# A sixteen-step recurrence chunk split in two halves, with one set of matrix products between them

## The reference

```python
for t in range(T):                       # state S: [B, H, DK, DV]
    S = S * a[t]                         # decay, one number for each value channel
    kS = k[t] @ S                        # what the state holds for this key
    S = S + outer(k[t], beta[t] * (v[t] - kS))
    o[t] = q[t] @ S
```

## Time and profile before

| what | value |
|---|---|
| device time, median of 3 runs | 3930.03 us (3925.61 to 3930.99) |
| profiled execution | 3934.55 us, its span 3932.7 us |
| recurrence, 64 chunks | about 104 to 2367 us of the span |
| mean granted PE clock, as a share of full | 0.895 |
| DVE busy over the span | 3225.6 us (82%) |
| PE busy over the span | 3308.3 us (84%) |
| POOL busy over the span | 2378.6 us (60%) |

### The profile page before, as it was taken

One profiled execution on the slowest core, in us unless ns is written; L12 is line 12 of the kernel. 1 busy time (PEld: TensorE's weight loads), 2 busy tenths in 40 slices (PEclk: granted clock), 3 DMA queues, 4 the chain that ended last, 5 costly groups with the idle time before them and its releaser, 6 DMA issues. The chain is left out here.

```text
span 3932.7 us, 110963 instructions
## 1 busy us (share of the span) xinstructions
PE 3308.3 (84%) x45505; PEld 2330.9 (59%) x45505; DVE 3225.6 (82%) x6024; ACT 2050.2 (52%) x4682; POOL 2378.6 (60%) x2981
## 2 busy tenths in 40 slices
PE   6788888888888888888888855759999899898989
PEld 4565666656656566565665634536666567655765
DVE  4899999999999999999999993048888778747884
ACT  4344444444444444444444423238888789728982
POOL 0777787777777887778777772430011088608860
PEclk9788888889888888888988875879999999999999
DMA  2111111111111111111111104100000011101110
GB/s 79 43 35 42 39 36 35 39 39 42 31 40 38 39 40 31 42 38 37 36 29 39 36 25 134 45 23 2 2 2 2 17 31 42 32 20 28 41 35 27
DMA packets 156105, 139.05 MB, mean 35 GB/s; under 512 B 65207, under 2 KB 108435, under 8 KB 155343
## 3 DMA queue, kind: packets, MB, share of 16 engines
q1 hardware_dynamic: 153294, 129.25, 11.9%
q0 software_dynamic: 2304, 2.71, 0.2%
HBM read 96.12 MB, written 16.82 MB: 29 GB/s over the span
## 5 line engine op out<-in xcount | busy, mean ns | idle before, releaser
L1133 DVE TENSOR_TENSOR a_tmp<-a_h,banks 128x128 f32<-128x128 f32 (+14 forms) x960 | 721.3, 751 | 33.9 <-POOL a_h L908 4.0
L1139 DVE TENSOR_REDUCE a_h<-a_tmp 128x64 f32<-128x128 f32 (+14 forms) x960 | 723.0, 753 | 26.3
L908 POOL TENSOR_TENSOR a_h<-a_h,a_a 128x128 f32<-128x128 f32 (+11 forms) x768 | 587.6, 765 | 135.9 <-DVE a_h L1139 121.0
L893 POOL TENSOR_TENSOR a_st<-a_st,a_ab 128x512 f32<-128x512 f32 x256 | 327.0, 1277 | 0.0
L740 ACT ACTIVATE a_va<-banks 128x512 f32<-128x512 f32 x128 | 138.0, 1078 | 354.9 <-PE banks L543 354.9
L529 PEld LDWEIGHTS banks<-a_xseg,a_w_k 128*128 128x128 f32 x2048 | 256.9, 208 | 54.5 <-DVE a_h L1139 35.3
L1984 ACT ACTIVATE c_s<-c_s,c_low 128x384 f32<-128x384 f32 (+1 forms) x512 | 266.3, 579 | 19.0 <-DVE c_low L1928 13.5
L2029 POOL TENSOR_TENSOR c_qm<-c_qT,c_heads 128x512 f32<-128x512 f32 x32 | 33.3, 1040 | 396.1 <-PE banks L1853 395.7
L529 PE MATMUL banks<-a_xseg,a_w_k 128*128 128x128 f32 x2048 | 262.9, 292 | 11.5 <-DVE a_h L1139 6.6
L1928 DVE CUSTOM_DVE_ANT_0 c_s<-banks,c_band 128x384 f32<-128x384 f32 (+1 forms) x512 | 245.4, 517 | 23.6 <-PE banks L1853 23.6
L657 PE MATMUL banks<-a_wt,a_kt 32*64 32x64 f32 x8192 | 157.3, 251 | 115.3 <-DVE a_wt L1157 111.4
(11 more groups left out here) (298 smaller groups left out, 8234.4 us busy)
## 6 DMA issues: line engine op xcount, KB each, us to landing
a_ab<-decays SPq DMA_DIRECT2D x512, 128.0 KB, 2.9
d_Vs<-d_V SPq DMA_DIRECT2D x128, 128.0 KB, 2.3
sent<-k_nothing SPq DMA_DIRECT2D x40, 64.5 KB, 2.3
b_xe<-sent SPq DMA_DIRECT2D x8, 322.5 KB, 3.4
a_xseg<-xn SPq DMA_DIRECT2D x32, 70.0 KB, 2.5
xn<-a_xnT SPq DMA_DIRECT2D x8, 256.0 KB, 2.7
a_xrow<-in_L_attn_x SPq DMA_DIRECT2D x128, 16.0 KB, 1.8
x<-a_xrow SPq DMA_DIRECT2D x128, 16.0 KB
```

Source lines behind the costliest of these rows:

```text
L893: e.tensor_tensor(sv, sv, self.ab[:, 8 * n:8 * n + 8, :], ALU.mult).then_inc(*self.s_decay.at((g, n)))
L908: e.tensor_tensor(self.history(ch, t + 1)[:, :, 0:t], self.history(ch, t)[:, :, 0:t], at, ALU.mult).then_inc(*self.s_hist.at((g, t)))
L1133: e.tensor_tensor(prod, both, gram, ALU.mult).then_inc(*step.at((g, t, "product")))
L1139: e.tensor_reduce(self.results(ch, t), prod, AX.X, ALU.add).then_inc(*step.at((g, t, "w")))
```

## The change

`HC` = 8 takes the place of `HOLD`. A chunk now has two halves of eight steps. In a step the history goes back only to the start of the step's half, so L1133 and L1139 have at most 64 x 8 elements and POOL's history at most 32 x 7. Step 8 isn't computed as a step. In its place `dve_cross` transposes the updates of the first half into `Wt`, PE multiplies them by the Gram matrix of the first half against the second (`pe_cross`, into banks 6 and 7), DVE transposes the products into a new tile `X`, and a product and a sum make the first four columns of the second half. POOL makes the other four (`pool_cross`) and corrects the query part (`pool_query`, now three instructions). DVE does the decays of steps 9 to 11 as it does those of 1 to 3. Running products of the decays now restart in the middle of a chunk, so `pool_cumulate` has 7 steps of twice the width instead of 15, and `pool_second_half` and `pool_first_half` multiply the middle's decay in. ACT makes a masked copy of the Gram matrix (`act_cross_gram`) and copies a second set of decay rows.

```diff
-HOLD = 9
+HC = CK // 2
 HAND = 4
...
+    def pe_cross(self, e, q, s, ch):
+        g, xb = 2 * s + ch, self.c.bank(6, 2)
+        q.wait_ge(self.s_gx, s)
+        q.wait_ge(self.s_wm, g)
+        for ct in range(NCT):
+            for par in range(2):
+                x, at = 16 * par + 2 * ct, par * BANK + ct * DK
+                for bi in range(NB):
+                    rows = slice(bi * SEG, (bi + 1) * SEG)
+                    t = e.matmul(xb[rows, at:at + DK], self.Gx[rows, :, :, 8 * par + ct].rearrange("p z t -> p (z t)"),
+                                 self.Wt[rows, x:x + 2, :].rearrange("p h i -> p (h i)"), start=True, stop=True)
+        t.then_inc(*self.s_x.at(g))
...
     def pe_carry(self, e, q, g):
+        q.wait_ge(self.s_xt, g)
...
-                q.wait_ge(self.s_step, (g, HOLD, "w"))
+            self.pe_cross(e, q, s, 0)
+            if more:
                 for half in range(2):
...
+                self.pe_project_rows(e, q, "v", nxt, 0)
+            self.pe_cross(e, q, s, 1)
             if older >= 0:
                 self.pe_out(e, q, older)
             if more:
-                q.wait_ge(self.s_step, (g, HOLD, "w"))
-                for half in range(2):
-                    self.pe_project_rows(e, q, "v", nxt, half)
+                self.pe_project_rows(e, q, "v", nxt, 1)
             self.pe_carry(e, q, g)
...
+    def act_cross_gram(self, e, q, s):
+        q.wait_ge(self.s_evac, ("gram", s, 1))
+        if s:
+            q.wait_ge(self.s_x, 2 * s - 1)
+        e.activation(self.Gx[:], self.G1[:], ACT.Identity, scale=self.cst["first_half"][:, 0:1],
+                     bias=self.cst["first_half"][:, 1:2]).then_inc(*self.s_gx.at(s))
...
+            lo = t // HC * HC
+            at = self.a2[s % 2][:, :, ch * CK + t:ch * CK + t + 1].broadcast_to([P, 32, t - lo])
             q.wait_ge(self.s_step, (g, t - 1, "w"))
-            if t > HAND:
+            if t > lo + HAND:
                 q.wait_ge(self.s_hist, (g, t - 1))
-            e.tensor_tensor(self.history(ch, t + 1)[:, :, 0:t], self.history(ch, t)[:, :, 0:t], at, ALU.mult).then_inc(
+            e.tensor_tensor(self.history(ch, t + 1)[:, :, lo:t], self.history(ch, t)[:, :, lo:t], at, ALU.mult).then_inc(
                 *self.s_hist.at((g, t)))
...
+    def pool_first_half(self, e, q, s, ch):
+        g, part, c1 = 2 * s + ch, self.W[ch][:, :, ch * CK:ch * CK + HC], ch * CK + CK - 1
+        q.wait_ge(self.s_wm, g)
+        e.tensor_tensor(part, part, self.dc[s % 2][:, :, c1:c1 + 1].broadcast_to([P, 32, HC]), ALU.mult).then_inc(
+            *self.s_hist.at((g, "whole")))
...
+    def pool_second_half(self, e, q, s, ch):
+        g, rest, c0 = 2 * s + ch, self.P2[:, :, HC:, 0], ch * CK
+        both = self.P2[:, :, HC:, :].rearrange("p i t z -> p i (t z)")
+        q.wait_ge(self.s_prep, (g, "sub"))
+        q.wait_ge(self.s_cum, (s, HC - 1))
+        e.tensor_tensor(both, both, self.dc[s % 2][:, :, c0 + HC - 1:c0 + HC].broadcast_to([P, 32, CK]),
+                        ALU.mult).then_inc(*self.s_rest.at((g, "middle")))
+        q.wait_ge(self.s_rest, (g, "middle"))
+        q.wait_ge(self.s_dk, (g, 1))
+        e.tensor_tensor(rest, rest, self.dk[:, :, HC:], ALU.mult).then_inc(*self.s_rest.at((g, "second")))
+        q.wait_ge(self.s_rest, (g, "second"))
+        q.wait_ge(self.s_bv, s)
+        e.tensor_tensor(rest, self.bv[:, :, c0 + HC:c0 + CK], rest, ALU.subtract).then_inc(*self.s_rest.at((g, "less")))
...
+    def pool_cross(self, e, q, s, ch):
+        g, x, at = 2 * s + ch, self.X[:, :, HC + HAND:CK], HC + HAND
+        q.wait_ge(self.s_xt, g)
+        e.tensor_tensor(x, x, self.dk[:, :, at:], ALU.mult).then_inc(*self.s_cross.at((g, "mul")))
+        q.wait_ge(self.s_cross, (g, "mul"))
+        for odd in range(2):
+            e.tensor_tensor(self.history(ch, at + odd)[:, :, at + odd::2], self.P2[:, :, at + odd::2, 0], x[:, :, odd::2],
+                            ALU.add).then_inc(*self.s_rest.at((g, "late", odd)))
...
     def pool_query(self, e, q, s, ch):
-        g, dc, P2 = 2 * s + ch, self.dc[s % 2], self.P2
-        q.wait_ge(self.s_cum, (s, CK - 1))
-        q.wait_ge(self.s_prep, (g, "sub"))
-        e.tensor_tensor(P2[:, :, :, 1], P2[:, :, :, 1], dc[:, :, ch * CK:(ch + 1) * CK],
-                        ALU.mult).then_inc(*self.s_pq.at(g))
+        g, of_q, last = 2 * s + ch, self.P2[:, :, :, 1], HC - 1
+        q.wait_ge(self.s_xt, g)
+        q.wait_ge(self.s_rest, (g, "middle"))
+        e.tensor_tensor(of_q[:, :, HC:], of_q[:, :, HC:], self.X[:, :, CK + HC:], ALU.subtract).then_inc(*self.s_cross.at((g, "q")))
+        q.wait_ge(self.s_cross, (g, "q"))
+        e.tensor_tensor(of_q, of_q, self.dc[s % 2][:, :, ch * CK:(ch + 1) * CK], ALU.mult).then_inc(*self.s_cross.at((g, "decayed")))
+        q.wait_ge(self.s_cross, (g, "decayed"))
+        e.tensor_tensor(of_q[:, :, last], of_q[:, :, last], self.X[:, :, CK + last], ALU.subtract).then_inc(*self.s_pq.at(g))
...
             self.pool_rest(e, q, s, 0)
-            self.pool_history(e, q, s, 0, HAND, 8)
+            self.pool_history(e, q, s, 0, HAND, HAND + 1)
+            self.pool_second_half(e, q, s, 0)
+            self.pool_history(e, q, s, 0, HAND + 1, HC)
             if old >= 0:
                 self.pool_centre(e, q, old, 0)
-            self.pool_history(e, q, s, 0, 8, 10)
+            self.pool_first_half(e, q, s, 0)
+            self.pool_cross(e, q, s, 0)
             if old >= 0:
                 self.pool_centre(e, q, old, 1)
-            self.pool_history(e, q, s, 0, 10, 12)
             self.pool_query(e, q, s, 0)
             for n in range(4):
-                self.pool_history(e, q, s, 0, 12 + n, 13 + n)
+                self.pool_history(e, q, s, 0, HC + HAND + n, HC + HAND + n + 1)
                 self.pool_decay(e, q, g, n)
             self.pool_prepare(e, q, s, 1)
...
+            self.pool_history(e, q, s, 1, HAND, HAND + 1)
+            self.pool_second_half(e, q, s, 1)
+            for t in range(HAND + 1, HC):
                 self.pool_history(e, q, s, 1, t, t + 1)
                 if more:
-                    self.pool_cumulate(e, q, nxt, 2 * (t - HAND), 2 * (t - HAND) + 2)
+                    self.pool_cumulate(e, q, nxt, t - HAND - 1, t - HAND)
+            if more:
+                self.pool_cumulate(e, q, nxt, 3, 5)
+            self.pool_first_half(e, q, s, 1)
+            self.pool_cross(e, q, s, 1)
+            if more:
+                self.pool_cumulate(e, q, nxt, 5, HC)
             self.pool_query(e, q, s, 1)
             for n in range(4):
-                self.pool_history(e, q, s, 1, 12 + n, 13 + n)
+                self.pool_history(e, q, s, 1, HC + HAND + n, HC + HAND + n + 1)
                 self.pool_decay(e, q, g, n)
             if more:
...
+            lo = t // HC * HC
+            if t == HC:
+                self.dve_cross(e, q, s, ch)
+                continue
+            hist, prod = self.history(ch, t), self.tmp[:, :, :, 0:t + 1 - lo]
+            both = hist[:, :, lo:t + 1].rearrange("p (o i) j -> p o i j", o=1).broadcast_to([P, 2, 32, t + 1 - lo])
+            gram = self.gbank[:, t - 1, :, lo:t + 1].rearrange("p z (o j) -> p z o j", o=1).broadcast_to([P, 2, 32, t + 1 - lo])
+            if t == lo + 1 and lo:
+                q.wait_ge(self.s_mid, (g, "add"))
+            elif t > 1:
                 q.wait_ge(step, (g, t - 1, "w"))
-            if t == HAND:
-                q.wait_ge(self.s_rest, (g, "sub", 1))
-            if t > HAND:
+            if t == lo + HAND:
+                q.wait_ge(self.s_rest, (g, "late" if lo else "sub", 1))
+            if t > lo + HAND:
                 q.wait_ge(self.s_hist, (g, t - 1))
             e.tensor_tensor(prod, both, gram, ALU.mult).then_inc(*step.at((g, t, "product")))
-            if t < HAND:
-                at = self.abank[:, t, :].rearrange("p (i o) -> p i o", o=1).broadcast_to([P, 32, t])
+            if t < lo + HAND:
+                at = self.abank[:, t, :].rearrange("p (i o) -> p i o", o=1).broadcast_to([P, 32, t - lo])
                 q.wait_ge(step, (g, t, "product"))
-                e.tensor_tensor(hist[:, :, 0:t], hist[:, :, 0:t], at, ALU.mult).then_inc(*step.at((g, t, "decay")))
+                e.tensor_tensor(hist[:, :, lo:t], hist[:, :, lo:t], at, ALU.mult).then_inc(*step.at((g, t, "decay")))
             q.wait_ge(step, (g, t, "product"))
...
+    def dve_cross(self, e, q, s, ch):
+        g, x = 2 * s + ch, self.X[:, :, HC:HC + HAND]
+        q.wait_ge(self.s_step, (g, HC - 1, "w"))
+        q.wait_ge(self.s_hist, (g, HC - 1))
+        if g:
+            q.wait_ge(self.s_u, (g - 1, 3))
+        e.transpose(self.Wt[:].rearrange("p x i -> p i x"), self.W[ch]).then_inc(*self.s_wm.at(g))
+        q.wait_ge(self.s_x, g)
+        if g:
+            q.wait_ge(self.s_pq, g - 1)
+        e.transpose(self.X[:], self.c.bank(6, 2).rearrange("p (x i) -> p i x", i=32)).then_inc(*self.s_xt.at(g))
+        q.wait_ge(self.s_xt, g)
```

(11 more changed lines are left out.)

67 lines of the change are left out of this document (37 added, 30 removed).

## The result

| | before | after |
|---|---|---|
| median of the runs, us | 3930.51 (3925.61 to 3937.14, 4 runs) | 4322.32 (4314.57 to 4334.36, 4 runs) |
| ratio after / before | | 1.0998 [1.0968, 1.1029] |
| span of the profiled execution, us | 3932.7 | 4332.6 |

The change makes the kernel 10% slower. The forecast was 4180 us with a range of 4090 to 4300: the direction was right and so was most of the way it comes about, but the size was not, and the result lies outside the range.

What follows compares the result with a forecast made beforehand. DVE was taken as the bound (94% busy in the recurrence), PE close behind. 29 segments x 8.3 us more, plus 8 for the others, made 249 on 3934.55: 4184, forecast as 4180 us, range 4090 to 4300.

Steps and rivals of the forecast that it cites:

- DVE is spared 5 to 6 us a chunk, and doesn't get the time: Shorter products and sums save DVE 5 to 6 us a chunk, but it must wait mid-chunk for PE, then POOL.
- POOL in the first half: POOL's second-half products delay history 5, so step 7 ends 11.2 instead of 9.9 us after the chunk's products transpose.
- The middle of an even chunk: PE reaches the middle products 14.6 us after the chunk's products transpose, they take 2.3, and X comes at 18.2.
- After X POOL sets the pace: From X to the update transpose POOL's queue takes 10.4 us in even chunks, where DVE alone would need 8.3.
- The odd chunk's value rows: Half of the value rows, 5.0 us, stands before the middle products, which PE reaches 18.6 us after the products transpose.
- The prediction's first rival: Half clock: middle products cost 3.36 instead of 2.3 us, value rows 7.3 instead of 5.0; 4312 us, chance 0.11.
- The sum: A segment takes 36.8 + 42.2 = 79.0 us against 70.67, 8.3 more in each of 29 segments.
- The SBUF lock: Behind X, DVE and POOL instructions reading SBUF may hold each other: DVE up to 0.9 us a chunk, POOL 0.6.
- PE in time: Rival: PE waits for DVE at the middle in both chunks, 1.3 us a segment more, 3972 us, chance 0.06.
- The point from which the change pays: X 16.0 us after the products transpose in both chunks with POOL as forecast, 17.9 if POOL keeps up.
- rival 3: Faster: PE arrives early and POOL keeps up, so only DVE counts; 5.1 us less a segment, 3767 us, chance 0.04.

Runs made afterwards that it cites:

- the third experiment: Kernel after the change, with POOL's three second-half products moved from between history 4 and 5 to behind history 7: 4312.3 us, 1.0973.
- second experiment: Kernel after the change, with POOL's centring and its last running products and decay moved ahead of the work that waits for X: 4226.7 us, 1.0760.
- the moves: Changed kernel with reordered POOL and PE queues (middle products earlier, POOL's side work moved), finally the output projection ahead of the Gram products: 4023.4 to 3929.6 us.
- The last kernel: Changed kernel with PE and POOL queues reordered, decay rows ahead of the turned output and segment input loaded one chunk earlier, run again: 3888.4 us, 0.9908.

## Why the prediction was right in kind and wrong in size

The step that failed is PE's way to the middle products in the odd chunk, the term of 5.0 us for the half of the value rows. It measured 7.9, because PE ran these rows at half clock behind its pauses. A second term, POOL's products behind X, was too small by 1.7 us a segment. The steps in order:

- *DVE is spared 5 to 6 us a chunk, and doesn't get the time.* Right: DVE's busy time fell from 3225.6 to 2885.8 us, 5.3 for each of 64 chunks, in the stage to 67% (about 70% forecast). Its idle time before L1253 is 3.8 us in even chunks (4 forecast) and 10.6 in odd ones (8 forecast).
- *POOL in the first half*: the updates were forecast to be turned at T + 13.1 and were at 13.3 and 13.2. POOL's time there was hidden, as the third experiment shows.
- *The middle of an even chunk*: PE was forecast at 14.6 and came at 14.3, the products at 2.3 and took 2.7, X at 18.2 and came at 18.3. Right.
- *After X POOL sets the pace*: right as a mechanism (second experiment), too small in size: 10.4 forecast and 10.9 measured in even chunks, 11.2 and 12.4 in odd ones. In the odd chunk the term "three running products of 128 elements and the last one in place of the centring (1.3 + 0.4)" was mis-sized: POOL's timeline behind X has 2.09 for the three and 0.42 for the last, and the first product of the query part is longer too (0.74 instead of 0.68). From X to history 12 that makes 6.3 us (1000.18 to 1006.47), where the forecast's durations add up to 5.2; this is nearly all of the 1.2. The 0.5 of the even chunk wasn't taken apart.

```profile
1000.18 0.56 POOL L1001 TENSOR_TENSOR a_cross<-a_cross,a_dk 128x128 f32<-128x128 f32 x1 [12.41 <-DVE a_cross L1253]
1000.82 0.71 POOL L1004 TENSOR_TENSOR a_h<-a_p,a_cross 128x64 f32<-128x64 f32 x2
1001.49 2.09 POOL L1049 TENSOR_TENSOR a_dc<-a_dc,a_a 128x128 f32<-128x128 f32 x3
1003.66 0.42 POOL L1060 TENSOR_TENSOR a_last<-a_dc 128x64 f32<-128x64 f32 x1
1004.03 0.74 POOL L1012 TENSOR_TENSOR a_p<-a_p,a_cross 128x256 f32<-128x256 f32 x1
1004.85 1.29 POOL L1014 TENSOR_TENSOR a_p<-a_p,a_dc 128x512 f32<-128x512 f32 x1
1006.47 0.45 POOL L944 TENSOR_TENSOR a_h<-a_h,a_a 128x128 f32<-128x128 f32 x1
```

- *The odd chunk's value rows*: this is the step that failed. Their start was right (13.6 forecast, 13.7 measured). "The half itself takes 5.0" was taken from one chunk of the trace before, where the mean of all odd chunks is 5.4; 7.9 is the mean after. PE reached the middle products at 21.6 instead of 18.6. The prediction's first rival had the right term (7.3) and the right cause, and it was given 0.11; the argument against it, that no idle time stands just before the middle products, looked at the wrong instruction, since the idle time stands before the value rows. That this rival's 4312 is near the 4322 is in part luck: the middle products took 2.7 and 2.1 us and not its 3.36, and POOL's 1.7 a segment made up for that. The range, too, took in only the middle products' share of a slow clock, and not the rows'.
- *The sum*: 83.6 a segment against 79.0. The value rows are 2.9 of these 4.6, the time from X to W 1.2 in the odd chunk and 0.5 in the even one. Times 29 segments that is 133 of the 142 us by which 4322 is above 4180.
- *The SBUF lock*: the small instructions behind X show DVE held by POOL, but not clearly POOL by DVE. Durations (ns, min/median/max):

```profile
L1255 DVE TENSOR_TENSOR a_cross<-a_cross,a_dk x64: 291/293/294, 124.8 to 2748.1; 128x128 f32<-128x128 f32 x64
L1001 POOL TENSOR_TENSOR a_cross<-a_cross,a_dk x64: 556/561/573, 124.9 to 2748.2; 128x128 f32<-128x128 f32 x64
L1258 DVE TENSOR_TENSOR a_h<-a_p,a_cross x64: 325/429/440, 125.1 to 2748.5; 128x128 f32<-128x128 f32 x64
```

DVE's product starts first and takes its 0.29 us, and POOL's starts 0.05 later. DVE's sum then takes 0.43, and it ends 0.15 us behind the end of POOL's product in each of the 64 chunks. By that order DVE's sum waits for the POOL instruction that had started first, as the Trainium skill, "SBUF — State Buffer", section "SBUF: two separate sides", has it for a DVE instruction with two SBUF inputs. So semaphores are not all that ties these two engines together. Whether POOL is held in its turn is still not shown: its product takes 0.56 where another tile's of that size took 0.46, 0.10 more, while 0.25 was left of DVE's product, and POOL's products of this size differ by tile (0.63 for the running decays). At most it is 0.1 us a chunk, not the 0.6 that was kept in the range.
- *Rivals*: PE in time (3972) is what the moves made of the kernel, 3929.6 to 4023.4. The point from which the change pays was put at X at T + 16.0 in both chunks. The kernel with the output projection moved has X at 16.0 in both and the time of the kernel before (1.0005), though its parts behind X are not the forecast ones. The last kernel has X at 15.6 in both and is faster, by 0.9% and not by the 4% of rival 3, since X to W takes 9.7 and 10.9 there, where the rival had 8.3 and 9.5.

## What to carry to other kernels

Less work on the engine that sets the pace doesn't pay by itself when it adds a round trip through another engine: find what stands ahead of the new instruction in that engine's in-order queue and what ends it, and move independent work behind it or into a pause. Price work on PE that follows a pause at the slow clock too, and put that price of all of it, not only of the new instructions, into the range. When PE's order is changed, look at the transfers that its new first instruction reads.

## What the runs showed of the hardware

- The granted clock follows PE's pauses inside a stage in which PE is busy for 81% (1653 of 2050 us): the value rows take 7.9 us behind pauses of 1.6 and 2.2 us in the mean, 7.2 behind one of 2.5, and 4.6 with the two filled by unread products. Adding work gained 77 us.
- Taking work away lowered the granted clock: 0.74 in the kernel before with one tap, 0.88 with all, and the time was the same within 0.2% (1.0014).
- A product of POOL over 128 elements of the running decays takes 0.62 to 0.69 us (L1049), not the 0.46 of the history's.
- A DVE sum over 512 elements with two SBUF inputs lasted 2.60 us beside two POOL products (1052.42 to 1054.92), where its median is 0.83:

```profile
1052.86 2.60 DVE L1279 TENSOR_TENSOR a_o<-a_p,a_h 128x512 f32<-128x512 f32 x1
```
